# Third routed layer: sorted tiles gathered by an inverse table instead of scattered, shared experts split around the routing

## The reference

```python
shared = _swiglu(x, wg_s, wu_s, wd_s) * RATIO          # 256 -> 256 -> 256
affinity = jax.nn.sigmoid(jnp.einsum('bsh,eh->bse', x, centroids))
biased = affinity + gate_bias
_, top_idx = jax.lax.top_k(biased, K)                  # K = 2 of E = 16
top_aff = jnp.take_along_axis(affinity, top_idx, axis=-1)
weights = top_aff / (top_aff.sum(-1, keepdims=True) + EPS)
mask = (jax.nn.one_hot(top_idx, E) * weights[..., None]).sum(-2)
for e in range(E):
    routed = routed + mask[..., e:e + 1] * _swiglu(x, wg[e], wu[e], wd[e])
return shared + routed
...
x = x + jnp.tanh(g_ffn[2]) * _L2_ffn_ref(_layernorm(x, axis=-1), ...)
```

## Time and profile before

| | us |
|---|---|
| three runs, least / median / most | 1188.04 / 1189.02 / 1189.30 |
| the profiled execution's own time | 1187.16 |
| its span in the trace | 1185.4 |
| PE busy (share of the span) | 945.1 (80%) |
| DVE busy | 660.6 (56%) |
| ACT busy | 438.3 (37%) |
| POOL busy | 383.5 (32%) |

### The profile page before, as it was taken

How to read it: one execution, slowest core, us unless ns; L and a number is a source line. 1 busy time by engine, 2 the same in 40 slices (tenths; PEclk the granted TensorE clock), 3 DMA queues, 4 the chain that set the end, 5 groups by cost and what they waited for, 6 DMA issues and landing times.

```text
span 1185.4 us, 18900 instructions
## 1 busy us (share of the span) xinstructions
PE 945.1 (80%) x6620; PEld 558.2 (47%) x6620; DVE 660.6 (56%) x1574; ACT 438.3 (37%) x722; POOL 383.5 (32%) x515
## 2 busy tenths in 40 slices
PE   3899985798299999777379726999989997199993
PEld 1455544687044456554247612344434444156662
DVE  5678753462679334777623358787887852211111
ACT  1366662111056313443014300466546575021220
POOL 5233204332631003442050061356555565200002
PEclk9999996989589999996589956699999999599997
DMA  6434524684543004542327530101210002700002
GB/s 183 122 102 146 175 82 186 187 291 153 125 113 83 1 1 121 173 95 67 142 102 227 170 95 15 41 2 42 108 42 2 2 3 108 267 21 23 14 14 80
DMA packets 112700, 116.32 MB, mean 98 GB/s; under 512 B 58824, under 2 KB 102408, under 8 KB 109576
## 3 DMA queue, kind: packets, MB, share of 16 engines
q1 hardware_dynamic: 101760, 96.62, 26.5%
q10 hardware_dynamic: 7776, 10.10, 2.6%
q0 software_dynamic: 3072, 8.39, 2.3%
HBM read 88.17 MB, written 30.67 MB: 100 GB/s over the span
## 4 chain that ended last, share of the span: by engine, by line
PE 47%; DVE 14%; DMA 7%; issue 7%; POOL 6%; ACT 2%; SPq 1%; POOLq 0%; ACTq 0%; DVEq 0%
PE psT L1523 7%; PE psT L1223 5%; PE psT L1374 5%; PE psB L1338 4%; DVE mxp L1929 4%; PE psB L1223 4%; PE psO L1418 3%; PE psB L1537 3%; PE psT L1486 2%; PE psB L1588 2%; PE psO L1408 2%; DMA scr_k_high<-sk 1%; PE psO L1406 1%; POOL scr_sorted L2354 1%; PE psB L1564 1%
## 5 line engine op out<-in xcount | busy, mean ns | idle before, releaser
L1929 DVE TENSOR_REDUCE mxp<-psB 128x1 f32<-128x512 f32 x256 | 163.7, 684 | 37.5 <-PE psB L1338 36.7
L1374 PE MATMUL psT<-whole 99*128 99x256 bf16 (+2 forms) x1024 | 153.1, 275 | 10.0 <-issue 9.0
L1933 DVE TENSOR_REDUCE mxp<-psB 128x2 f32<-128x512 f32 x192 | 123.5, 684 | 31.6 <-PE psB L1344 31.2
L1675 ACT ACTIVATE Pt<-psT,ln 128x1024 f32<-128x1024 f32 x96 | 106.7, 1114 | 63.8 <-PE psT L1374 62.7
L1374 PEld LDWEIGHTS psT<-whole 99*128 99x128 bf16 (+2 forms) x1024 | 96.5, 102 | 54.1 <-issue 21.5
L1675 ACT ACTIVATE Pt<-psT 128x1024 f32<-128x1024 f32 x96 | 98.1, 1024 | 58.3 <-PE psT L1374 56.6
L1338 PE MATMUL psB<-whole 96*128 96x512 bf16 x256 | 96.2, 427 | 24.3 <-DMA whole<-scr_q 13.9
L2283 POOL TENSOR_TENSOR rstd<-vare,cst 128x1 f32<-128x1 f32 x64 | 35.8, 562 | 231.3 <-DVE vare L1836 231.0
L1344 PE MATMUL psB<-whole 96*128 96x256 bf16 x384 | 78.0, 306 | 36.0 <-DMA whole<-scr_q 20.3
L1523 PE MATMUL psT<-whole,qf 128*128 x176 | 82.3, 612 | 0.6 <-ACT qf L1729 0.6
L2342 POOL TENSOR_SCALAR nb_t<-Pt 128x1024 f16<-128x1024 f32 x64 | 67.2, 1051 | 39.5 <-ACT Pt L1675 37.4
(11 more groups left out here) (323 smaller groups left out, 1743.8 us busy)
## 6 DMA issues: line engine op xcount, KB each, us to landing
whole<-in_w SPq DMA_DIRECT2D x32, 512.0 KB, 5.2
whole<-in_w SPq DMA_DIRECT2D x5, 3072.0 KB, 10.3
xn<-scr_sorted ACTq DMA_DIRECT2D x42, 128.0 KB, 2.2
scr_q<-sq SPq DMA_DIRECT2D x48, 96.0 KB, 2.2
whole<-scr_q SPq DMA_DIRECT2D x24, 192.0 KB
whole<-scr_k SPq DMA_DIRECT2D x24, 192.0 KB, 3.5
scr_sorted_out<-xn SPq DMA_DIRECT2D x31, 128.0 KB, 2.4
scr_k<-sk SPq DMA_DIRECT2D x32, 96.0 KB, 1.9
```

Of the source, the lines that this page charges most:

```text
L1374: ins = pe.matmul(psT[:, s.n % 2, i * A.T:(i + 1) * A.T], lhsT=k_at[:, h * kw + s.c * P:h * kw + (s.c + 1) * P], rhs=q_at[:, h * A.T:(h + ...
L1675: act.activation(p_slot(A, s.p)[:, 0:4 * A.T], psT[:, s.n % 2, 0:4 * A.T], ACT.Exp, bias=bias, scale=scale).then_inc(T_used[s.n % 2], 1)
L1929: dve.tensor_reduce(mxp[:, s.un.g % 2, at:at + 1], psB[:, s.n % BANKS, :], AX.X, ALU.max).then_inc(bank_used[s.n % BANKS], 1)
L1933: dve.tensor_reduce(mxp[:, s.un.g % 2, at:at + 2], psB[:, s.n % BANKS, :].rearrange("p (h n) -> p h n", h=2), AX.X, ALU.max).then_inc(bank ...
```

## The change

Tokens. While the attention before runs, each batch's normalised rows are also stored, in order, to a new scratch tensor `scr_tokens` (`xnd`), by SP (a step `tokens` behind each `fn` of layer 2).

The inverse table. Instead of writing rows to their slots, the kernel computes for each slot which token it holds. Each pair's slot is split into its tile (0 to 31) and its lane (0 to 127). For each of the 16 columns of pairs (2 choices x 8 batches), DVE makes a one-hot row of the lane over 128 (`slot_low`) and one of the tile over 32 (`slot_hit`), the latter once times the token's lane and once times its batch's base (`slot_tile`). Sixteen bfloat16 matmuls, `invert`, add up `slot_low` transposed times `slot_tile`: a 128x64 result whose two halves add up to the token number of every slot. DVE adds them and casts to `token`. Empty slots get token 0, and nobody reads their results. A row of positions, `iota`, comes from one matmul.

The loads. `tload(t)` on POOL gathers the 128 rows of tile t from `scr_tokens` by `token[:, t]`, straight into `sx`. Tiles 0 to 3 come after the table; tile t + 4 comes as soon as `tx(t)` is done on PE. The 16 scatters and ACT's 31 loads are gone.

The shared experts. `gate_up2(0, ...)` stands ahead of `route`, `gate_up2(1, ...)` behind it, silu and product are steps of their own, `rank2` is the second half of the old routing, and the eight `down2` stand behind the first four `tload`. Their hidden values move to another part of `whole`, silu to `nb_t`.

```diff
@@ turned(layer)
                 add("fn", xn=xs[0])
+                if layer == 2:
+                    add("tokens", xn=xs[0])
@@ sorted_pairs()
         add("w3load", item="w_at3")
-        route(2, take("M"))
-        for b in range(NB):
-            add("scatter2", b=b)
-        shared = dense(2)
-        add("t_load")
+        add("iota", m=take("M"))
+        for ch in range(2):
+            gate_up2(0, ch)()
+        m_route = take("M")
+        route(2, m_route)
+        for tg in range(2):
+            for ch in range(2):
+                if tg:
+                    gate_up2(1, ch)()
+                silu2(tg, ch)
+                if not tg:
+                    gated2(0, ch)
+        add("rank2", m=m_route)
+        add("invert", m=take("M"))
+        for ch in range(2):
+            gated2(1, ch)
         tiles = {}
+
+        def tload(t):
+            add("tload", i=t, m=tiles[t - 4].m_x if t >= 4 else None)
+        for t in range(4):
+            tload(t)
+        for tg in range(2):
+            for tc in range(4):
+                down2(tg, tc)()
+        shared = last["down2"]
 
         def tx(t):
             tiles[t] = Record(i=t)
             tiles[t].m_x = add("tx", i=t, m=take("M")).m
+            if t + 4 < TILES2:
+                tload(t + 4)
@@ sync
+                elif s.kind == "tokens":
+                    sp.wait_ge(xn_ready, s.xn.i + 1)
+                    sp.dma_start(xnd[s.xn.b * P:(s.xn.b + 1) * P, :], xn[:, s.xn.b, :]).then_inc(tokens_out, 16)
@@ tensor
                 elif s.kind == "tx":
                     dst = m_begin(s.m)
-                    pe.wait_ge(sorted_in[s.i % 4], 16 * (s.i // 4 + 1))
+                    pe.wait_ge(tile_in[s.i % 4], 16 * (s.i // 4 + 1))
+                elif s.kind == "iota":
+                    dst = m_begin(s.m)
+                    pe.matmul(dst[:, 0:P], lhsT=const("ones"), rhs=const("before"), start=True, stop=True
+                              ).then_inc(bank_ready[s.m % BANKS], 1)
+                elif s.kind == "invert":
+                    dst = m_begin(s.m)
+                    pe.wait_ge(slots_set, 1)
+                    for c in range(16):
+                        ins = pe.matmul(dst[:, 0:64], lhsT=slot_low[:, c, :], rhs=slot_tile[:, c, :, :],
+                                        start=(c == 0), stop=(c == 15))
+                    ins.then_inc(bank_ready[s.m % BANKS], 1)
@@ scalar
-                elif s.kind == "t_load":
-                    act.wait_ge(scattered2, 16 * 2 * NB)
-                    for i in range(4):
-                        act.dma_start(sx[:, i, :], xd[i * P:(i + 1) * P, :]).then_inc(sorted_in[i], 16)
                 elif s.kind == "tx":
...
-                    if s.i + 4 < TILES2:
-                        act.dma_start(sx[:, s.i % 4, :], xd[(s.i + 4) * P:(s.i + 5) * P, :]).then_inc(sorted_in[s.i % 4], 16)
+                elif s.kind == "silu":
+                    turn(act, T_ready, s.un.n)
+                    act.activation(silu_slot(2, s.un.sg), psT[:, s.un.n % 2, 0:512], ACT.Silu).then_inc(silu_done, 1)
@@ vector, step rank2 (the lines ahead of this are those of the old routing, unchanged)
+                    place = late[:, 264:280].rearrange("p (k b) -> p k b", k=2)
+                    tile_of, low_of = r8[:, 0:2, :], r8[:, 4:6, :]
...
+                    link(dve.tensor_scalar(tile_of, place, 1.0 / P, 0.5 / P - 0.5, ALU.mult, ALU.add))
+                    link(dve.tensor_scalar(tile_of, tile_of, MAGIC, MAGIC, ALU.add, ALU.subtract))
+                    link(dve.scalar_tensor_tensor(out=low_of, in0=tile_of, scalar=-float(P), in1=place, op0=ALU.mult,
+                                                  op1=ALU.add))
...
+                    for k in range(2):
+                        dve.tensor_tensor(lows[:, k], iota.unsqueeze(1).to_broadcast([P, NB, P]),
+                                          low_of[:, k, :].unsqueeze(2).to_broadcast([P, NB, P]), ALU.is_equal)
+                        link(dve.tensor_tensor(hits[:, k], const("tiles").unsqueeze(1).to_broadcast([P, NB, 32]),
+                                               tile_of[:, k, :].unsqueeze(2).to_broadcast([P, NB, 32]), ALU.is_equal))
+                    link(dve.tensor_scalar(by_lane, slot_hit, lane, None, ALU.mult))
+                    for k in range(2):
+                        ins = dve.tensor_tensor(by_batch[:, k], hits[:, k],
+                                                const("base").unsqueeze(2).to_broadcast([P, NB, 32]), ALU.mult)
+                    ins.then_inc(slots_set, 1)
...
+                elif s.kind == "invert":
+                    turn(dve, bank_ready, s.m)
+                    dve.tensor_copy(tmp2[:, 64:96], m_slot(s.m)[:, 0:32]).then_inc(dve_chain, 1)
...
+                    dve.tensor_tensor(tmp2[:, 96:128], tmp2[:, 64:96], m_slot(s.m)[:, 32:64], ALU.add
+                                      ).then_inc(bank_used[s.m % BANKS], 1)
+                    evacuated(dve, s.m)
+                    dve.tensor_copy(token[:, :], tmp2[:, 96:128]).then_inc(inverted, 1)
@@ gpsimd
-                elif s.kind == "scatter2":
-                    if s.b == 0:
-                        pool.wait_ge(routed2, 1)
-                    for k in range(2):
-                        pool.indirect_dma_start(xd, bass.IndirectOffsetOnAxis(ap=idx[:, k, s.b:s.b + 1].bitcast(U32), axis=0),
-                                                xn[:, s.b, :], None).then_inc(scattered2, 16)
+                elif s.kind == "tload":
+                    if s.i == 0:
+                        pool.wait_ge(inverted, 1)
+                        pool.wait_ge(tokens_out, 16 * NB)
+                    if s.m is not None:
+                        turn(pool, bank_ready, s.m)
+                    pool.indirect_dma_start(sx[:, s.i % 4, :], None, xnd,
+                                            bass.IndirectOffsetOnAxis(ap=token[:, s.i:s.i + 1].bitcast(U32), axis=0)
+                                            ).then_inc(tile_in[s.i % 4], 16)
```

More of the change, by code:

```diff
@@ L694, in ffn1_rest, with gate_up2, f, gated2 @@
             + [(gate_up1(1, ch), FFN1[4] + (FFN1[5] - FFN1[4]) * ch / n) for ch in range(n)]
[L696 to L720, removed]
+    def gate_up2(tg, ch):
+        blk = ffn_blocks(2)[0]
+        def f():
+            xt = [s for s in steps if s.kind == "xt" and s.xn.b == tg * 4 + 3][-1]
+            assert xt.layer == 2
+            g = add("gu", layer=2, blk=blk, tg=tg, ch=ch, width=blk.widths[ch], h=tg, m=xt.m, n=take("T"), sg=take("sg"))
+            last["T2", tg], last["gu2", tg, ch] = g.n, g
+        return f
+    def gated2(tg, ch):
+        add("gm", un=last["gu2", tg, ch])
+    def silu2(tg, ch):
+        add("silu", un=last["gu2", tg, ch])
+    def down2(tg, tc):
+        blk = ffn_blocks(2)[0]
+        def f():
+            s = add("down", layer=2, blk=blk, tg=tg, tc=tc, h=tg, last_T=last["T2", tg], n=take("S"))
+            last["down2"] = s.n
+        return f
     before = []
@@ L845, in flamingo @@
         idx = sb("idx", [P, 2, NB], I32)
+        token = sb("token", [P, 32], I32)
         psB = pb("psB", [P, BANKS, 512])
@@ L879, in flamingo @@
         dk = [nc.dram_tensor(f"scr_k{i}", [3, 2 * P, 256], BF16).ap() for i in range(2)]
+        xnd = nc.dram_tensor("scr_tokens", [NT, D], F32).ap()
         dk1 = nc.dram_tensor("scr_k1_all", [NB, P, 3, 256], BF16).ap()
@@ L949, in flamingo @@
         combined = sem("combined")
+        tile_in = [sem(f"tile_in{i}") for i in range(4)]
         sorted_in = [sem(f"sorted_in{i}") for i in range(4)]
         sorted_out = [sem(f"sorted_out{i}") for i in range(4)]
-        scattered2, scattered3 = sem("scattered2"), sem("scattered3")
+        tokens_out, slots_set, inverted = sem("tokens_out"), sem("slots_set"), sem("inverted")
+        scattered3 = sem("scattered3")
         gathered2 = [sem(f"gathered2_{b}") for b in range(NB)]
-        routed2, hidden2 = sem("routed2"), sem("hidden2")
+        hidden2 = sem("hidden2")
         table_made = sem("table_made")
@@ L973, in silu_slot @@
         def silu_slot(layer, i):
-            return nb_t[:, i % 2, :] if layer == 1 else sg[:, i % 2, :]
+            return nb_t[:, i % 2, :]
         def uses2(i):
@@ L1748, in _ @@
                                    ).then_inc(T_used[s.n % 2], 1)
-                elif s.kind == "gu":
+                elif s.kind == "gu" and s.layer == 1:
                     w = s.width
                     turn(act, T_ready, s.n)
-                    sc = col("gs1", s.ch, w) if s.layer == 1 else 1.0
-                    act.activation(silu_slot(s.layer, s.sg)[0:w, :], psT[0:w, s.n % 2, 0:512], ACT.Silu, scale=sc
+                    act.activation(silu_slot(1, s.sg)[0:w, :], psT[0:w, s.n % 2, 0:512], ACT.Silu, scale=col("gs1", s.ch, w)
                                    ).then_inc(silu_done, 1)
+                elif s.kind == "silu":
+                    turn(act, T_ready, s.un.n)
```

(10 more changed lines are left out.)

86 lines of the change are left out of this document (53 added, 33 removed).

## The result

The changed kernel takes 1179.48 us (median of 15 runs, 1172.95 to 1187.15); the kernel before, in 15 runs among them, 1185.60 (1182.36 to 1189.30). The ratio is 0.9941, 95% interval 0.9919 to 0.9962: about 7 us less, interval 4.5 to 9.6. The forecast was 9.7 us less than the kernel before.

What follows compares the result with a forecast made beforehand. DVE's routing plus POOL's scatter set the time to tile 0, then PE bounds the loop. Terms -8.7 - 1.8 + 0.8 = -9.7 us took 1187.16 to 1177.5, with 1.86 added 1179.3; eight-in-ten range 1174.5 to 1185.

Steps and rivals of the forecast that it cites:

- the loop term: In the loop over sorted tiles: each gather lands 0.8 us later, which shows once beside the key loads, +0.8 us.
- signs of being wrong: PE waiting over 3 us for tile loads in the loop, clock 0.50 in down products, or DVE's list after 600.
- Steps 1 to 3: Around the routing: iota +0.9 us; first half of gate and up free in PE's hole; DVE's gated products (1.45 us) hidden.
- Step 5: DVE's new operations ahead of the inverse table: 5.6 us, lists there at 598.2; bounds 3.2 and 8 us.
- Step 6: PE's second half of gate and up, behind the routing: 6.9 us at full clock, up to 9.7, costing nothing.
- Step 7: Inverse table's sixteen matmuls on PE: 2.0 us (1.0 to 3.5), done at 600.2; tile 0's gather there at 605.
- Step 8: Ahead of the loop: down products end last, at 607.8, tile 0 turned 8.7 us earlier; full clock then gives 1.8.
- The first rival: Up to the loop: PE stays at half clock, tile 0 turned 6.7 us later than before, total 1196.5 us; chance 0.05.
- the gather becomes the loop's bound: In the loop: landings near 8 us under load make tiles take 2.0 us, +8.4, net -1.3; chance 0.13.
- The token stores: In SyncE's queue during the attention before: eight stores wait in time it has, costing nothing.

Runs made afterwards that it cites:

- e7: The kernel before with only the shared experts split around the routing; old scatters and ScalarE loads kept, no token stores or table: ratio 1.0002 to the kernel before.
- e1: The changed kernel with tile loads issued by ScalarE as direct loads of whole batches (wrong tokens, no gather): ratio 0.9884 to the kernel before.
- e4: The changed kernel with eight tile buffers instead of four, gathers issued eight tiles ahead: ratio 0.9942 to the kernel before.
- e6: The changed kernel with the token list set to zero, so every slot of all 31 tiles reads row 0: one run, 1183.57 us.
- e5: The changed kernel with its 1920 empty slots pointed at 128 different rows, real tokens in true order: ratio 0.9894 to the kernel before.
- e3: The changed kernel with the eight key loads moved from tiles 3 to 24 of the loop to its end (24 to 31): one run, 1184.13 us.

## Why the prediction was right or wrong

The mechanism held up to the loop, and the direction too; 9.7 us were forecast, 7.0 measured (4.5 to 9.6). The step that failed is the loop term. From the logits to tile 30 the forecast is 9.7 us as well, and the two profiles give 8.2: 12.6 won ahead of the loop where 10.5 were forecast (8.7 + 1.8), 4.4 lost in it where 0.8 were. The two errors are of opposite sign and cancel in part; that is luck. So is it that the time itself, 1179.3, came within 0.2 us of the median 1179.48: it was counted from 1189.02, the median of three runs of the kernel before, and over 15 runs that kernel has 1185.60. One of the prediction's own signs of being wrong also came up: PE waits for tile loads in the loop for 3.1 us, and the sign was over 3.

- Steps 1 to 3. Iota cost +0.9 in the forecast. From logits to the routing's first operation it was 1.33 us before (574.50 to 575.83) and 2.24 after (577.15 to 579.39): 0.91. The first half of gate and up took 9.67 us, ended in the hole, and left a hole of 2.02 us (2.0 in the forecast). The rank started 14.24 us after the logits, forecast 14.45; the products hid it, as said.
- Step 5. Both compares of 1024 took 1.22 us as extrapolated, two-byte outputs bringing nothing. The product of 512 with two-byte input and one number per lane took 0.35, not 0.72; the sum was 5.0 us instead of 5.6.
- Step 6. After that hole the clock did fall: it was 1.00 in the hole and 0.50 from 591 to 594, 16 records took 8.59 us instead of 6.9, and it still cost nothing, the products being done as the lists came. In e7, with a hole of 1.46 us, the clock stayed at 1.00 and the same 16 took 7.10. The length of the hole does not decide alone: in e1 it fell after 1.94 us (8.70), in e4 and e6 it stayed at 1.00 after 2.49 and 2.55 us (7.10 both). The Trainium skill's rule that idle time sends the array to half rate ("TensorE: Matmul & The Clock Gate", Part 1) agrees in kind with the fall in this trace, from 1.00 to 0.50 behind a hole of 2.02 us. The price of the fall was 1.5 us (8.59 less 7.10), all of it covered. The first rival (half clock up to the loop) did not come about: the stretches show 0.91 and 1.00.
- Step 7. The sixteen table matmuls took 0.63 us, not 2.0: together far less than 16 times one alone, so the price of one matmul alone (219 ns) was the wrong neighbour.
- Step 8. PE's down products were last, not the gather, with both stalls on DVE. T0 came after 32.04 us; forecast 33.3. Won 9.9 instead of 8.7, and at tile 3 another 2.65 instead of 1.8.
- The loop: +0.8 forecast, 4.36 measured. The step priced a gather by its landing at a quiet time (2.8 us) and let that time be all that it adds. The term that was missing is the queue time of a gather: with half of all slots at row 0 it is 12.2 engine-us for a gather where distinct rows need 7.8, and stores and key loads pay as well. With the repetition taken out (e5), 48.69 against 48.35 remain: 0.3 us, and the step would have held. The rival "the gather becomes the loop's bound" named the place and a size (landings near 8 us, up to +8.4; 24 tiles of 0.37 us more would be 8.9). Its cause, the load that the queues have anyway and POOL's issue time on top, is not the one: under the same load and with the same POOL issues e5's gathers landed in 3.4 us (median), 6.5 at most, where the changed kernel's took 4.6 and 8.0. The Trainium skill's figure for the first byte of software descriptors (its page "DMA: Bandwidth & Descriptors") would have made the term smaller still, 0.4 us for a landing; here the least landings differ by 0.7 (2.7 us for POOL's gathers, 2.0 for ACT's loads).
- The token stores cost nothing that shows: the last logits start between 572.21 and 577.15 us in the eight profiled kernels that have them, at 573.42 and 574.50 in the two that have not (e7 and the kernel before). A cost of a few us would hide in that spread; e5's total, 0.9894 with 11.6 us won from the logits to tile 30, leaves little room for one.

What stays open: why reading one row of DRAM many times takes more engine time than reading many rows. The runs show that it does and how much, not the part of the memory that it comes from. Nor do they show that any one row would do: only row 0 was repeated. And e3 and e6 rest on a single run each.

## What to carry to other kernels

Here padding cost what its addresses cost: point the unused slots of a gather at different rows, not all at row 0, and price an indirect load by the engine time that it takes in a full queue, not by its landing in an empty one. Where a second chain ends about as late as the one that a change shortens, or is made to by the change itself, the change alone shows nothing; look for the second before judging the first. Before adding buffers, look at who else is in the queue: deeper prefetch moved the waits from gathers to stores and gained nothing.

## What the hardware showed that was not expected

- A gather of 128 rows of 1 KB took 19 to 20 engine-us of queue time in the loop when all 128 rows were the same and under 8 when they differed, at nearly the same count of packets, and it held up unrelated transfers: the stores' median landing was 4.7 us in e6 against 3.1 in e5.
- POOL's issue time doesn't show it: in e3 its median is 946 ns for the gathers that landed in 2.7 us (median) and 944 for those that landed in 5.3 to 7.5.
- After a stall of PE the clock is a second cost: in e4 one of 4.42 us was followed by about 4.6 us of work at 0.50. But a hole of 2.0 us brought it down in the changed kernel, and holes of 2.5 us in e4 and e6 did not.
- Sixteen accumulating bf16 matmuls of 64 columns, each with a new weight tile of 128x128, took 0.63 us together, 39 ns each, where one short bf16 matmul alone has a record of 219 ns.
